# A graph layer and a routed feed-forward layer on one core: another order of the beginning, and the stores of the experts' outputs issued by SP

## The chip, the cores and the metric

The kernel runs on one core of a Trainium2 chip. The metric is the device time of one execution in microseconds (us). The core has a matrix engine (TensorE, PE in the profile), a vector engine (VectorE, DVE), an activation engine (ScalarE, ACT), a general engine (GpSimd, POOL) and SyncE (SP), which here does nothing but issue transfers. Each engine runs its own list of instructions in order; they wait for each other through semaphores.

## What is computed

The input `x` is 128 graphs of 64 nodes with 128 features, that is 8192 rows, and `adj` a 64x64 matrix for each graph. There are two layers, each behind a layer norm and a residual sum:

```python
def gnn(x, adj, ...):            # first layer
    h = layer_norm(x, ln_gamma, ln_beta)
    conv = (adj @ h) @ W_rel + b_rel + h @ W_root
    return x + relu(conv)
def ffn(x, ...):                 # second layer, 8 experts, the 2 best of each row
    scores = x @ Wg.T + bg
    combine = softmax over the two highest scores, 0 elsewhere
    for e in range(8):
        out += combine[e] * (relu(x @ W1[e].T + b1[e]) @ W2[e].T + b2[e])
x = x + gnn(_layernorm(x), adj, ...)
x = x + ffn(_layernorm(x), ...)
```

## The kernel before, in words

The 8192 rows are 64 tiles of 128 rows. Four tiles are a quad (16 quads, number n), and the quads fall into five groups (g) of 8, 16, 16, 16 and 8 tiles. Group 0 is quads 0 and 1, group 1 is quads 2 to 5.

A quad goes through the graph layer like this: `stats_in` and `scales_in` (DVE) make the scales of the layer norm; `norm_in` (DVE) or `h0_make` (ACT) normalizes into N; PE transposes (`h0_transpose`), ACT copies (`hT_copy`), PE multiplies (`relation`), ACT copies (`u_copy`), PE multiplies with the adjacency (`convolve`, semaphore conv_done). `plus_norm` (ACT) adds the normalized input into X, `residual` (DVE) adds the relu, `stats_out`, `scales_out_first` and `scales_out_last` make the next scales, `norm_out` normalizes, `split_high` (ACT) and `split_low` (DVE) make two half-precision parts XHL, `xn_transpose`, `xnT_copy` and `score` give the gate's scores, and `scores` (DVE, L466) copies them to LG.

For a group, DVE then picks the two best experts of each row (`route_first`, `route_second`), PE counts (`rank`), and DVE computes where each row goes (`route_slots`, `route_rows`, which ends with IDX, L543) and which expert each block has (`route_blocks`). POOL scatters the rows of the group, sorted by expert, to the DRAM tensor `rows` with two indirect DMAs for each tile (`scatter`, L317), and after the experts gathers their outputs from `yrows` in the same way (`gather`, L330). POOL's order is scatter 0, scatter 1, gather 0, scatter 2, scatter 3, gather 1, scatter 4, gathers 2, 3, 4. A scatter waits for zeros that SP wrote into `rows` (`zero_rows`).

The sorted rows are worked on in 84 blocks of 256 rows (number p; 12, 20, 20, 20 and 12 by group). For block p, PE computes `hidden(p)` (L990 to L992) as soon as SP has brought the rows in transposed (XT, `load_rows`, L244, four chunks of two blocks each), ACT and DVE make the two halves HH and HL (`high_half` L791, `low_half` L571), PE computes `output(p)` (L1006 to L1019) after `hidden(p+1)`, ACT copies it to YB (`y_copy`, L799), and once a chunk of two blocks is copied its 256 KB are stored to `yrows` (`store_y`). YB holds three chunks. The order of everything on each engine is written out by hand; the tables START, STATS, ROUTE and COMBINE say beside which block the later quads and groups get their steps.

Before the block loop comes the beginning. On PE it is: the graph layer of quads 0 to 3 up to `convolve`, the scores of quads 0 and 1, then the first experts' weights (`four_whole`, `four_rest`: 8 experts in two halves through the banks WB, each answered by `four_high` and `four_low` on ACT), then `first_half(4, 5)`, then the transposes and scores of quads 2 to 5. The second weights are split by `second_high` (ACT) and `second_low` (DVE, L580), one 512-column piece for each expert. `output(0)` waits for all eight of them (w2lo_made).

SP issues its transfers in one order too: `load_rows(ch)` of a chunk waits, for a group's first chunk, until the scatter of that group has landed, and from the fifth chunk on until the chunk that had the place has been read (hb_done).

Of the kernel before, what the change touches and what calls it, by code (L numbers as in the profile page):

```python
# [76 lines left out]
def build(nc, x, adj, wgn, w1, w2, b1, b2, kf, kh, out):  # L77
    ctx = ExitStack()
    with ctx:
# [71 lines left out]
        WB = 2 * [PA, PB, PH[0], PH[1]]  # L151
# [74 lines left out]
        def _(sp):  # L226
# [22 lines left out]

            def zero_rows(b):  # L250
                sp.wait_ge(zero_made, 1)
                sp.dma_start(rows[b].rearrange("(p n b) d -> p n (b d)", p=P, n=3),
                             ZERO.unsqueeze(1).to_broadcast([P, 3, ZW])).then_inc(zero_out[b], 16)
# [16 lines left out]
            zero_rows(0)  # L270
            for n in (4, 5):
                sp.wait_ge(conv_done, n - 3)
                load_adj(n)
            zero_rows(1)
# [9 lines left out]
            for ch in range(len(CH)):  # L284
# [5 lines left out]
                for n, at in COMBINE.items():  # L290
                    if ch == CB[at] + 6:
                        store_out(n)
            for n in range(NQ):
# [54 lines left out]
        def _(dve):  # L348
# [59 lines left out]
            def norm_in(n):  # L408
                g = group_of(n, Q0)
                if n >= 4:  # L410
                    dve.wait_ge(xnT_done, n - 3)
                    dve.wait_ge(xhi_made, n - 3)
                for k in range(GT):
# [211 lines left out]
            split_low(1)  # L625
            scores(0)
# [3 lines left out]
            norm_in(4)  # L630
            route_slots(0)
            route_rows(0)
            route_blocks(0)

            dve.wait_ge(b1hi_made, 1)
            nc.vector.scalar_tensor_tensor(B1L[:, :], B1F[:, :], W1S, B1H[:, :], ALU.mult, ALU.subtract).then_inc(b1lo_made, 1)
            dve.wait_ge(bt_made, 1)
            nc.vector.scalar_tensor_tensor(B2[32:33, :], B2F[32:33, :], YS / 64.0, BT[32:33, :],
                                           ALU.mult, ALU.subtract).then_inc(b2_made, 1)
            pair_of_quads(2)  # L640
            second_low(0, 1)
            split_low(2)
            split_low(3)
            second_low(1, 2)
            scores(2)
            second_low(2, 3)
            scores(3)
            pair_of_quads(4)
            second_low(3, 6)
            split_low(4)  # L650
            split_low(5)
            second_low(6, 7)
            scores(4)
            second_low(7, 8)
            scores(5)
            route_first(1)
            route_second(1)
# [47 lines left out]
        def _(act):  # L705
# [95 lines left out]
            def store_y(ch):  # L801
                g, r, w = chunk_rows(ch)
                act.wait_ge(y_made, CH[ch][1] + CH[ch][2])
                act.dma_start(yrows[g][r, :].rearrange("(k p) d -> p k d", p=P),
                              YB[:, ch % YR * CW:ch % YR * CW + w].rearrange("p (k d) -> p k d", d=P)).then_inc(y_out[ch % YR], 16)

# [22 lines left out]
            for n in (0, 1):  # L829
                xnT_copy(n)  # L830
            plus_norm(3)
            h0_make(5)
            four_high(0)
            exp_gap(0)
            four_low(0)
            four_high(4)
            four_low(4)
            act.wait_ge(b1_in, 16)
            nc.scalar.mul(B1H[:, :], B1F[:, :], W1S).then_inc(b1hi_made, 1)
            act.wait_ge(b2_in, 32)  # L840
            nc.scalar.activation(B2[0:1, :], B2F[0:1, :], ACT.Copy, scale=YS / 64.0).then_inc(b2_made, 1)
            nc.scalar.activation(BT[32:33, :], B2F[32:33, :], ACT.Copy, scale=YS / 64.0).then_inc(bt_made, 1)
# [4 lines left out]
            second_high(0, 4)  # L847
            norm_out(3)
            for n in (2, 3):
                split_high(n)  # L850
            for n in (2, 3):
                xnT_copy(n)
            for n in (4, 5):
                plus_norm(n)
            second_high(4, 8)
# [3 lines left out]
            for n in (4, 5):  # L859
                xnT_copy(n)  # L860
            act.wait_ge(b2_made, 2)

            for p in range(NP):
# [4 lines left out]
                for ch, (g, first, n) in enumerate(CH):  # L868
                    if p == first + n + 1:
                        store_y(ch)  # L870
# [23 lines left out]
            for ch, (g, first, n) in enumerate(CH):  # L894
                if first + n + 1 >= NP:
                    store_y(ch)
# [259 lines left out]
```

## Time and profile before

| what | value |
|---|---|
| median of 3 runs | 740.11 us (738.97 to 742.23) |
| the profiled execution | 739.89 us, its span 738.0 us |
| TensorE busy | 397.4 us, 54% of the span |
| VectorE, ScalarE, GpSimd busy | 310.2, 241.7 and 250.0 us |
| mean DMA rate | 81 GB/s |
| indirect DMAs of GpSimd | 256: 128 scatters, 128 gathers |

The page of the profile cuts the span into 40 equal slices and gives one digit for the busy share of each engine in each. The timeline lists instructions in order of time. A view by windows gives the busy time of each engine, with the number of its instructions, between two moments. "remote" or "another core or an unknown queue" stands where an engine waited and the profile names no engine that released it at that moment.

### The profile page before, as it was taken

Reading aid. Unit: us, or ns where it says so; the run is one execution under the profiler, and the core shown is the slowest. Engines: PE = TensorE matmul, PEld = TensorE weight load, DVE = VectorE, ACT = ScalarE, POOL = GpSimd, SP = SyncE. Lnnn points to the kernel's source line nnn. Section 1 sums busy time; section 2 is a strip of 40 time slices with the busy share of each in tenths; the row PEclk is TensorE's granted clock in tenths of the full one; section 3 lists DMA queues with packets and bytes.
Section 4 is the critical chain, followed back from the end, with each engine's and each line's share of the span. In section 5 each row is a group of like instructions: output and inputs, shape, how many; then the busy total and the mean of one; then the engine's idle time right before and its main releaser. Section 6 shows DMA issues by size and latency. Waiting matters only on the chain.

```text
span 738.0 us, 12242 instructions
## 1 busy us (share of the span) xinstructions
PE 397.4 (54%) x3927; PEld 332.7 (45%) x3927; DVE 310.2 (42%) x1113; ACT 241.7 (33%) x519; POOL 250.0 (34%) x263
## 2 busy tenths in 40 slices
PE   4873652199728505987211139964801999415910
PEld 4652540198618404875100039853701887314700
DVE  6773870067707403568400005761400753203651
ACT  3875310178425202852100027621300553102300
POOL 2043047400340672002777700044375000672053
PEclk9996585599868855999655559995955899756965
DMA  9934022132221211133111123232331442421231
GB/s 306 368 142 116 0 54 82 33 73 66 55 64 38 78 50 50 36 79 73 50 53 53 50 61 73 64 75 61 73 82 43 112 117 62 104 53 47 67 106 53
DMA packets 86540, 59.48 MB, mean 81 GB/s; under 512 B 57426, under 2 KB 78546, under 8 KB 85844
## 3 DMA queue, kind: packets, MB, share of 16 engines
q1 hardware_dynamic: 56756, 31.23, 14.7%
q0 software_dynamic: 8192, 16.79, 8.0%
q10 hardware_dynamic: 21536, 10.69, 6.1%
q8 instruction: 38, 0.62, 0.3%
q14 instruction: 18, 0.15, 0.1%
HBM read 19.61 MB, written 28.38 MB: 65 GB/s over the span
## 4 chain that ended last, share of the span: by engine, by line
PE 40%; another core or an unknown queue 23%; issue 19%; DVE 9%; ACT 5%; POOL 2%; DMA 1%; ACTq 0%; SPq 0%; DVEq 0%; POOLq 0%
PE PH L990 6%; PE PY L1014 5%; PE PY L1019 5%; PE PY L1015 5%; PE PH L992 5%; PE PH L991 4%; PE PY L1006 2%; POOL YG L330 2%; PE PB L911 1%; ACT N L734 1%; DVE STI L384 1%; PE PA L919 1%; DVE HL L571 1%; PE PA L920 1%
## 5 line engine op out<-in xcount | busy, mean ns | idle before, releaser
L571 DVE SCALAR_TENSOR_TENSOR HL<-PH,HH 128x512 f16<-128x512 f32 (+1 forms) x168 | 108.4, 674 | 293.0 <-ACT HH L791 244.5
L317 POOL DMA_INDIRECT rows<-XHL,IDX x128 | 123.9, 968 | 264.5 <-DVE IDX L543 227.0
L330 POOL DMA_INDIRECT YG<-yrows,IDX x128 | 121.8, 951 | 211.8 <-DMA yrows<-YB 173.9
L791 ACT ACTIVATE HH<-PH 128x512 f16<-128x512 f32 (+1 forms) x168 | 95.6, 582 | 145.3 <-remote 95.8
L1015 PE MATMUL PY<-W2H,HL 128*128 x652 | 122.6, 231 | 18.5 <-issue 18.4
L1014 PE MATMUL PY<-W2H,HH 128*128 x652 | 122.6, 231 | 10.9 <-issue 10.7
L990 PE MATMUL PH<-XT,W1H 128*128 128x256 f16 (+1 forms) x396 | 107.1, 273 | 26.6 <-issue 24.8
L799 ACT ACTIVATE YB<-PY 128x256 f32<-128x256 f32 x84 | 31.8, 378 | 272.7 <-remote 167.2
L992 PE MATMUL PH<-XT,W1L 128*128 128x256 f16 (+1 forms) x396 | 106.1, 271 | 20.5 <-issue 20.5
L1019 PE MATMUL PY<-W2L,HH 128*128 x652 | 106.6, 231 | 18.0 <-issue 18.0
L991 PE MATMUL PH<-XT,W1H 128*128 128x256 f16 (+1 forms) x396 | 106.3, 271 | 17.4 <-issue 17.4
L1006 PE MATMUL PY<-B,KH 128*128 x99 | 27.0, 272 | 110.5 <-issue 62.7
L1015 PEld LDWEIGHTS PY<-W2H,HL 128*128 128x128 f16 x652 | 67.8, 104 | 15.8 <-issue 15.0
L1014 PEld LDWEIGHTS PY<-W2H,HH 128*128 128x128 f16 x652 | 67.4, 103 | 15.7 <-issue 13.2
L1019 PEld LDWEIGHTS PY<-W2L,HH 128*128 128x128 f16 x652 | 57.1, 104 | 23.2 <-issue 22.7
L1006 PEld LDWEIGHTS PY<-B,KH 128*128 128x128 f16 x99 | 10.0, 101 | 120.3 <-issue 118.8
L990 PEld LDWEIGHTS PH<-XT,W1H 128*128 x396 | 41.2, 104 | 46.8 <-issue 37.4
L992 PEld LDWEIGHTS PH<-XT,W1L 128*128 x396 | 40.8, 103 | 25.3 <-issue 20.5
L991 PEld LDWEIGHTS PH<-XT,W1H 128*128 x396 | 40.9, 103 | 23.1 <-issue 19.2
L590 DVE SCALAR_TENSOR_TENSOR X<-YG,PR,X 128x128 f32<-128x128 f32 x128 | 36.2, 347 | 17.2 <-DMA YG<-yrows,IDX 16.6
L460 DVE SCALAR_TENSOR_TENSOR XHL<-N,XHL 128x512 f16<-128x512 f32 x16 | 10.8, 690 | 47.3 <-issue 30.7
L727 ACT ACTIVATE X<-X,SHI,SC 128x128 f32<-128x128 f32 x64 | 26.1, 483 | 0.0
(186 smaller groups left out, 517.8 us busy)
## 6 DMA issues: line engine op xcount, KB each, us to landing
yrows<-YB ACTq DMA_DIRECT2D x37, 256.0 KB, 2.7
rows<-XT SPq DMA_DIRECT2D x2, 2496.0 KB, 15.5
YG<-in_w SPq DMA_DIRECT2D x2, 2048.0 KB, 11.8
out<-X SPq DMA_DIRECT2D x16, 256.0 KB
X<-in_x SPq DMA_DIRECT2D x3, 1024.0 KB, 5.5
ADJ<-in_adj SPq DMA_DIRECT2D x32, 64.0 KB, 3.2
rows<-XHL,IDX POOLq DMA_INDIRECT x128
YG<-yrows,IDX POOLq DMA_INDIRECT x128
```

The costliest lines, as they stand in the source:

```text
L317: nc.gpsimd.indirect_dma_start(rows[g % 2], bass.IndirectOffsetOnAxis(ap=IDX[:, col:col + 1], axis=0), XHL[:, src:src + 2 * P].bitcast(F32 ...
L330: nc.gpsimd.indirect_dma_start(YG[g % 2][:, dst:dst + P], None, yrows[g], bass.IndirectOffsetOnAxis(ap=IDX[:, col:col + 1], axis=0)).then_ ...
L571: nc.vector.scalar_tensor_tensor(layer(HL[:, at:at + 2 * BW], p), layer(PH[p % 2 * 2 + h][:, :], p), 0.0, layer(HH[:, at:at + 2 * BW], p), ...
L590: ins = nc.vector.scalar_tensor_tensor(tile(X, t), y, PR[:, pr:pr + 1], tile(X, t), ALU.mult, ALU.add)
L791: nc.scalar.activation(layer(HH[:, at:at + 2 * BW], p), layer(PH[p % 2 * 2 + h][:, :], p), ACT.Relu).then_inc((hia_made, hib_made)[h], 1)
L990: nc.tensor.matmul(o, wh, hi, start=True, stop=False)
L991: nc.tensor.matmul(o, wh, lo, start=False, stop=False)
L992: last = nc.tensor.matmul(o, wl, hi, start=False, stop=True)
L1006: nc.tensor.matmul(PY[:, k * n * P:(k + 1) * n * P], KH[:, H_B2M:H_B2M + P], b2, start=True, stop=False, skip_group_check=True)
L1014: nc.tensor.matmul(o, HH[:, at:at + P], wh, start=False, stop=False, skip_group_check=True)
L1015: nc.tensor.matmul(o, HL[:, at:at + P], wh, start=False, stop=False, skip_group_check=True)
L1019: last = nc.tensor.matmul(o, HH[:, at:at + P], wl, start=False, stop=c == C - 1, skip_group_check=True)
```

## The change

The diff does five things:

1. `store_y` moves from ACT to SP. ACT issued the store of a chunk one block after its last copy, behind the two `high_half` of that block. SP issues it as soon as the copy is made; its loop over chunks (`next_chunk`) is cut into the first four chunks and then, block by block, the load of chunk ch+4 and the store of chunk ch.
2. On SP, `zero_rows(0)` stands after the adjacency loads of quads 4 and 5.
3. On PE, the graph layer of quads 4 and 5 up to `convolve` stands before the weights; the weights' banks (WB) and the waits that protect them are others.
4. On DVE, `norm_in(4)`, `residual`, `stats_out` and `scales_out` of quads 2 and 3 move around the routing of group 0; `residual` to `norm_out` of quads 4 and 5 stand before the scores of quads 2 and 3; six of the eight `second_low` and the low part of B2 stand after `route_second(1)`.
5. On ACT, the steps of quads 4 and 5 stand before `four_high(0)` or between the weights; the parts of B2 and six of the eight `second_high` come last.

```diff
 PH = [pb(f"PH{k}") for k in range(4)]
 PY = pb("PY")
 PA, PB, PC = pb("PA"), pb("PB"), pb("PC")
-WB = 2 * [PA, PB, PH[0], PH[1]]
+WB = [PB, PH[1], PH[3], PC, PB, PH[1], PY, PH[2]]
 
 def banks(n):
 
...
         sp.wait_ge(combined, n + 1)
         sp.dma_start(out[:, n * GW:(n + 1) * GW], X[:, n * GW:(n + 1) * GW]).then_inc(out_done, 16)
 
+    def store_y(ch):
+        g, r, w = chunk_rows(ch)
+        sp.wait_ge(y_made, CH[ch][1] + CH[ch][2])
+        sp.dma_start(yrows[g][r, :].rearrange("(k p) d -> p k d", p=P),
+                      YB[:, ch % YR * CW:ch % YR * CW + w].rearrange("p (k d) -> p k d", d=P)).then_inc(y_out[ch % YR], 16)
+
     def zero_rows(b):
         sp.wait_ge(zero_made, 1)
         sp.dma_start(rows[b].rearrange("(p n b) d -> p n (b d)", p=P, n=3),
...
     sp.dma_start(YG[1][:, :], w2[:, :]).then_inc(w2_in, 16)
     for r in (0, 32):
         sp.dma_start(B2F[r:r + 1, :], b2[:, :]).then_inc(b2_in, 16)
-    zero_rows(0)
     for n in (4, 5):
         sp.wait_ge(conv_done, n - 3)
         load_adj(n)
+    zero_rows(0)
     zero_rows(1)
 
     sp.wait_ge(b1hi_made, 1)
...
         load_x(g)
     for b in range(2):
         sp.wait_ge(zero_out[b], 16)
-    for ch in range(len(CH)):
+    def next_chunk(ch):
         load_rows(ch)
         for n, at in START.items():
             if ch == CB[at] + 2:
...
         for n, at in COMBINE.items():
             if ch == CB[at] + 6:
                 store_out(n)
+
+    for ch in range(XR):
+        next_chunk(ch)
+
+    for p in range(NP + 1):
+        for ch, (g, first, n) in enumerate(CH):
+            if p == first + n - 1 and ch + XR < len(CH):
+                next_chunk(ch + XR)
+            if p == first + n:
+                store_y(ch)
     for n in range(NQ):
         if n not in COMBINE or CB[COMBINE[n]] + 6 >= len(CH):
             store_out(n)
...
         if n >= 4:
             dve.wait_ge(xnT_done, n - 3)
             dve.wait_ge(xhi_made, n - 3)
+            dve.wait_ge(xlo_made, n - 3)
         for k in range(GT):
             t = n * GT + k
             at = 2 * T0[g] + GS[g] + t - T0[g]
...
     pair_of_quads(0)
     split_low(0)
     split_low(1)
+    norm_in(4)
     scores(0)
     scores(1)
     route_first(0)
     route_second(0)
-    norm_in(4)
+    residual(2)
+    stats_out(2, 0)
     route_slots(0)
     route_rows(0)
+    residual(3)
+    stats_out(3, 1)
+    scales_out_first(2, 2)
+    scales_out_last(2, 2)
+    norm_out(2)
     route_blocks(0)
 
     dve.wait_ge(b1hi_made, 1)
     nc.vector.scalar_tensor_tensor(B1L[:, :], B1F[:, :], W1S, B1H[:, :], ALU.mult, ALU.subtract).then_inc(b1lo_made, 1)
+    for i in range(2):
+        residual(4 + i)
+        stats_out(4 + i, i)
+    split_low(2)
+    split_low(3)
+    scales_out_first(4, 2)
+    scales_out_last(4, 2)
+    norm_out(4)
+    second_low(0, 2)
+    scores(2)
+    scores(3)
+    split_low(4)
+    split_low(5)
+    scores(4)
+    scores(5)
+    route_first(1)
+    route_second(1)
     dve.wait_ge(bt_made, 1)
     nc.vector.scalar_tensor_tensor(B2[32:33, :], B2F[32:33, :], YS / 64.0, BT[32:33, :],
                                    ALU.mult, ALU.subtract).then_inc(b2_made, 1)
-    pair_of_quads(2)
-    second_low(0, 1)
-    split_low(2)
-    split_low(3)
-    second_low(1, 2)
-    scores(2)
-    second_low(2, 3)
-    scores(3)
-    pair_of_quads(4)
-    second_low(3, 6)
-    split_low(4)
-    split_low(5)
-    second_low(6, 7)
-    scores(4)
-    second_low(7, 8)
-    scores(5)
-    route_first(1)
-    route_second(1)
+    second_low(2, 8)
 
     for p in range(NP):
         for n, at in START.items():
...
         at = ch % YR * CW + (p - CH[ch][1]) * BW
         nc.scalar.mul(YB[:, at:at + width(p)], PY[:, 0:width(p)], 1.0 / YS).then_inc(y_made, 1)
 
-    def store_y(ch):
-        g, r, w = chunk_rows(ch)
-        act.wait_ge(y_made, CH[ch][1] + CH[ch][2])
-        act.dma_start(yrows[g][r, :].rearrange("(k p) d -> p k d", p=P),
-                      YB[:, ch % YR * CW:ch % YR * CW + w].rearrange("p (k d) -> p k d", d=P)).then_inc(y_out[ch % YR], 16)
-
     act.wait_ge(b2_zero, 1)
 
     nc.scalar.activation(IDLE[:, :], B2[:, 0:1], ACT.Identity)
...
         split_high(n)
     for n in (0, 1):
         xnT_copy(n)
+    h0_make(5)
     plus_norm(3)
-    h0_make(5)
-    four_high(0)
-    exp_gap(0)
-    four_low(0)
-    four_high(4)
-    four_low(4)
-    act.wait_ge(b1_in, 16)
-    nc.scalar.mul(B1H[:, :], B1F[:, :], W1S).then_inc(b1hi_made, 1)
-    act.wait_ge(b2_in, 32)
-    nc.scalar.activation(B2[0:1, :], B2F[0:1, :], ACT.Copy, scale=YS / 64.0).then_inc(b2_made, 1)
-    nc.scalar.activation(BT[32:33, :], B2F[32:33, :], ACT.Copy, scale=YS / 64.0).then_inc(bt_made, 1)
     for n in (4, 5):
         hT_copy(n)
     for n in (4, 5):
         u_copy(n)
-    second_high(0, 4)
+    exp_gap(0)
+    plus_norm(4)
+    act.wait_ge(b1_in, 16)
+    nc.scalar.mul(B1H[:, :], B1F[:, :], W1S).then_inc(b1hi_made, 1)
+    four_high(0)
+    plus_norm(5)
+    four_low(0)
     norm_out(3)
     for n in (2, 3):
         split_high(n)
+    four_high(4)
+    four_low(4)
+    second_high(0, 2)
     for n in (2, 3):
         xnT_copy(n)
-    for n in (4, 5):
-        plus_norm(n)
-    second_high(4, 8)
     norm_out(5)
     for n in (4, 5):
         split_high(n)
     for n in (4, 5):
         xnT_copy(n)
+    act.wait_ge(b2_in, 32)
+    nc.scalar.activation(B2[0:1, :], B2F[0:1, :], ACT.Copy, scale=YS / 64.0).then_inc(b2_made, 1)
+    nc.scalar.activation(BT[32:33, :], B2F[32:33, :], ACT.Copy, scale=YS / 64.0).then_inc(bt_made, 1)
+    second_high(2, 8)
     act.wait_ge(b2_made, 2)
 
     for p in range(NP):
...
             exp_gap(1)
         high_half(p, 0)
         high_half(p, 1)
-        for ch, (g, first, n) in enumerate(CH):
-            if p == first + n + 1:
-                store_y(ch)
         for n, at in START.items():
             if p == at + 5:
                 xnT_copy(n)
...
             if p == at + 2:
                 exp_gap(g)
     y_copy(NP - 1)
-    for ch, (g, first, n) in enumerate(CH):
-        if first + n + 1 >= NP:
-            store_y(ch)
 
 @block.tensor
 def _(pe):
...
 
     def weight_whole(c):
 
-        if c >= 4:
+        if c == 3:
+            pe.wait_ge(rank_used, 1)
+        if c in (4, 5):
             pe.wait_ge(wlo_made, c - 3)
+        if c >= 6:
+            pe.wait_ge(conv_read, c - 3)
         nc.tensor.matmul(WB[c][0:P - 1, :], KF[:, K_M:K_M + P - 1], YG[0][:, c * HID:(c + 1) * HID],
                          start=True, stop=True).then_inc(w_done, 1)
 
...
         xn_transpose(n)
     for n in (0, 1):
         score(n)
+
+    pe.wait_ge(score_made, 2)
+    for n in (4, 5):
+        h0_transpose(n)
+    for n in (4, 5):
+        relation(n)
     pe.wait_ge(kh_in, 16)
+    rank(0)
+    for n in (4, 5):
+        convolve(n)
     pe.wait_ge(w1_in, 16)
-
-    pe.wait_ge(score_made, 2)
     four_whole(0)
-    rank(0)
     four_rest(0)
     four_whole(4)
     four_rest(4)
     pe.wait_ge(wlo_made, 8)
-    first_half(4, 5)
     for n in (2, 3):
-        if n == 3:
-            pe.wait_ge(rank_used, 1)
         xn_transpose(n)
     for n in (2, 3):
         score(n)
```

## Rows read from the trace of the kernel before

**Rows 1.** The page: slices of PE and POOL; the zeros' stores.
```profile
PE   4873652199728505987211139964801999415910
POOL 2043047400340672002777700044375000672053
...
rows<-XT SPq DMA_DIRECT2D x2, 2496.0 KB, 15.5
```
**Rows 2.** By windows: stretch; busy us and instructions of PE, PEld, DVE, ACT, POOL; clock; DMA; GB/s.
```profile
44.43:50.80 6.37, 3.24 (x24) 2.70 (x25) 4.33 (x15) 5.56 (x10) 4.99 (x5) 1.00 0.42 122
50.80:61.00 10.20, 5.04 (x40) 4.66 (x39) 6.97 (x32) 5.33 (x12) 7.69 (x8) 0.97 0.66 262
98.92:107.20 8.28, 6.60 (x58) 5.55 (x58) 7.09 (x33) 0.38 (x1) 6.45 (x7) 0.65 0.15 48
107.20:143.96 36.76, 4.91 (x16) 1.49 (x16) 1.38 (x2) 1.20 (x2) 24.28 (x26) 0.56 0.22 62
143.96:193.76 49.80, 44.73 (x518) 42.03 (x519) 35.89 (x149) 37.60 (x87) 0.00 (x1) 0.95 0.28 64
353.00:435.60 82.60, 9.52 (x41) 4.66 (x41) 6.98 (x22) 3.11 (x7) 55.56 (x59) 0.53 0.16 47
```
**Rows 3.** Timeline of POOL (start, duration): scatter 0's first and last, scatter 1's.
```profile
44.43 1.13 POOL L317 DMA_INDIRECT rows<-XHL,IDX  x1 [39.58 <-DVE IDX L543]
63.86 0.96 POOL L317 DMA_INDIRECT rows<-XHL,IDX  x1 [0.30 <-issue]
98.92 0.96 POOL L317 DMA_INDIRECT rows<-XHL,IDX  x1 [34.10 <-DVE IDX L543]
138.13 0.96 POOL L317 DMA_INDIRECT rows<-XHL,IDX  x1 [0.30 <-issue]
```
**Rows 4.** Timeline of PE and ACT in the two scatters.
```profile
64.34 0.37 PE L926 MATMUL PC<-KF,N 128*128 128x128 f32 x1 [0.96 <-issue]
67.45 0.59 ACT L758 COPY T<-PH 128x512 f32<-128x512 f32 x1 [6.19 <-remote]
110.02 0.27 PE L1019 MATMUL PY<-W2L,HH 128*128 x2 [1.18 <-issue]
143.96 0.38 ACT L799 ACTIVATE YB<-PY 128x256 f32<-128x256 f32 x1 [26.26 <-remote]
```
**Rows 5.** Timeline of DVE: group 0's IDX; a pair's residual, scales, norm_out; second_low.
```profile
43.96 0.17 DVE L543 CAST IDX<-SLF 128x16 int32<-128x16 f32 x1
71.81 0.68 DVE L424 SCALAR_TENSOR_TENSOR X<-PA,X 128x512 f32<-128x512 f32 x1
78.40 1.11 DVE L453 TENSOR_SCALAR N<-X,SCO,SHO 128x127 f32<-128x127 f32 x4
79.43 1.88 DVE L580 SCALAR_TENSOR_TENSOR W2L<-YG,W2H 128x512 f16<-128x512 f32 x3
48.40 1.27 DVE L638 SCALAR_TENSOR_TENSOR B<-HL,HH 1x1024 f16<-1x1024 f32 x1 [1.66 <-issue]
```
**Rows 6.** Timeline: the last scores before the loop on PE and DVE, group 1's IDX.
```profile
83.33 1.85 PE L935 MATMUL PH<-WF,T 128*128 128x8 f32 x8
85.22 0.19 DVE L466 COPY LG<-PH 128x32 f32<-128x32 f32 x1 [0.92 <-PE PH L935]
98.46 0.18 DVE L543 CAST IDX<-SLF 128x32 int32<-128x32 f32 x1
```
**Rows 7.** Timeline: a group's last copy and its store, twice; SP's second store of zeros.
```profile
187.32 0.28 ACT L799 ACTIVATE YB<-PY 128x128 f32<-128x128 f32 x1
190.54 0.37 ACTq L804 DMA_DIRECT2D yrows<-YB  x1
703.75 0.28 ACT L799 ACTIVATE YB<-PY 128x128 f32<-128x128 f32 x1 [1.42 <-PE PY L1019]
704.06 0.37 ACTq L804 DMA_DIRECT2D yrows<-YB  x1
...
22.55 3.95 SPq L252 DMA_DIRECT2D rows<-XT  x1
```

## The prediction

> **What bounds the kernel now.** I began with the slices of the page [rows 1]. PE is busy for about half of the span, yet not evenly: its digits are 9 in some stretches and 0 or 1 in others, and wherever POOL's digits stay at 6 or 7 for two slices and more, PE's fall to 0 to 2. So I cut the span at POOL's bursts of indirect DMAs. After scatter 1 begins at 98.92 us, PE does 58 matmuls in 8.28 us, and then 16 in 36.76 us; in the longest burst the rest is 41 in 82.60 us, against 518 in 49.80 us in a stretch without a burst [rows 2]. The timeline shows what the waiting is: PE's last matmul of block 2's output starts at 110.02, and ACT, which waits for nothing else, copies that output at 143.96, 5.8 us after the start of the burst's last DMA (138.13) [rows 3, 4]. So inside a burst signals from PE arrive later and later, and PE itself comes to a crawl after some 60 matmuls. That number recurs: 24 + 40 in scatter 0 up to 61.0 us, 58 in scatter 1 [rows 2]. What it is in the chip I can't read from these rows; that it happens is enough.
>
> The time is therefore the work between bursts, plus some 60 matmuls' worth in each, plus the rest of each burst. 256 indirect DMAs follow each other every 1.26 us or so (19.43 us for 15 steps, 39.21 for 31 [rows 3]), and the diff changes neither their number nor their grouping. What it can change is how early scatter 1 starts: from there on all instructions are the same but for the stores. The first question is thus when IDX of group 1 is made (98.46 to 98.64), which follows the scores of quad 5 at DVE (done 85.41) by 13.2 us of routing without a gap, the burst 0.28 us behind [rows 3, 6]. Call the end of those last scores S; before, S = 85.4.
>
> **Beginning, up to scatter 0.** PE takes the eight transposes, relations and convolutions of quads 4 and 5 before the weights; DVE trades `norm_in(4)` (behind group 0's routing) for `residual(2)` and its statistics. Group 0's slots wait on DVE's own chain and on `rank(0)`, which PE now does before the weights' first half rather than behind it. I count IDX of group 0 about 0.5 us earlier (43.5 instead of 44.1) and scatter 0's first DMA at 43.9 instead of 44.43 [rows 3, 5]. It could be 1 us later if ACT's copies hold `rank(0)`; both ends stay in the range. `zero_rows(0)` goes to about 22.5 us, where `zero_rows(1)` is issued now [rows 7], and has 21 us to land, where the zeros took 15.5 [rows 1]: at no cost. If that cover were gone, scatter 0 would start late by the lack.
>
> **Scatter 0 and what stands beside it.** The burst ends as before 19.4 us behind its start, and the engines it held were released at 67.45, 3.6 us behind its last DMA's start [rows 3, 4]; now that is 43.9 + 19.4 + 3.6 = 66.9. Before, the burst had beside it the convolutions of quads 4 and 5, and PE's allowance of some 60 matmuls was used up by them and the first transposes: at 64.34 it was still at quad 3's transposes. Behind the release came everything of a pair's chain: copies, scores 2 and 3, residual, scales, norm_out, scores 4 and 5: 18 us, from 67.45 to 85.41 [rows 4, 6].
>
> Now PE has beside the burst only some 18 matmuls of the weights, 8 transposes and 16 scores of quads 2 and 3, and 8 transposes of quads 4 and 5, 50 in all; 16 of quads 4 and 5's scores are left. DVE's chain needs nothing from PE after `convolve(5)`. From IDX at 43.5 it is residual and statistics of quad 3 (1.6), scales (3.5), norm_out (1.1), blocks of group 0 (2.7 with B1), residual and statistics of 4 and 5 (3.1), two split_low (1.3), scales (3.5), norm_out (1.1): 61.4 us. The parts come from the pair at 71.81 to 79.5, which is 6.6 us up to norm_out and 1.1 for it [rows 5]. So DVE is through about 5 us before the release. I expect quad 4 and 5's transposes issued but their signals held to 66.9. Then: ACT's copy 0.6, two scores of 1.9 at the half clock [rows 4, 6], DVE's copy 0.2 and hand-overs of 0.2: S = 71.4. That is 14.0 earlier. Bounds: if no signal is late, the chain itself ends at 66.8 (earliest S, 67); if ACT gets the scales of quads 4 and 5 only at the release, norm_out and split_high (2.8 us) come on top, S = 74.2. I take the middle case, since held signals are what the rows of scatter 0 show, and the half clock what PE has after idling.
>
> **What comes back.** The low part of B2 (1.27) and six `second_low` (1.88 for three, 3.8) now stand between `route_second(1)` and the first `low_half`, and so ahead of `route_slots(1)` on the same in-order engine [rows 5]: 5.1 us, of which nothing lies beside other work, because DVE has no gap from S to IDX. Behind it waits POOL, and `output(0)` on PE. ACT's six `second_high` lie beside DVE's routing and cost nothing. `hidden(0)` starts 4 us later relative to S, since it waits for B2, but PE idles there: `output(0)` waits for DVE in either case.
>
> Scatter 1 starts at 71.4 + 13.5 + 5.1 = 90.0 instead of 98.92: **8.9 us earlier**. At its start the loop stands where it stood (the same blocks done, since DVE's order from the first `low_half` on is the same), so all behind moves with it.
>
> **The stores by SP.** ACT loses 42 issues of 0.37 us [rows 7], which cost its activations nothing visible, as they were issued beside them; and ACT isn't the bound in the loop: 37.60 of 49.80 us, PE 44.73 [rows 2]. SP gets them in the order in which their causes occur: the load of chunk ch+4 needs `hidden` of a chunk's last block, the store its copy one block later, the next load the next `hidden`. At a group's end the store was 2.9 us behind the copy (190.54 against 187.60), and SP can issue it at once [rows 7], so gathers 0 to 3 start up to 3 us earlier. That gives nothing: a burst that begins earlier finds PE as much less far, and costs the same. At the very end the store already followed at once (704.06 against 704.03) [rows 7], and there alone it would count. I take 0, between -3 (if the earlier gathers shorten something that I don't see) and +3.
>
> Here the Trainium skill speaks against the change: DMA: Bandwidth & Descriptors, Queues, rings and completion order, says that SP and ACT own one ring each on every DMA engine, that a ring is worked through in order and that an engine takes turns between rings. A store on SP's ring would stand behind the transposing load and adjacency loads issued before it, where on ACT's it took its turn. No row here shows the two on one ring. By it the gathers come later than I say by some transfer, which changes the sum only at the end of the kernel, where SP has no loads left.
>
> **Sum.** Profiled execution 739.89 - 8.9 = 731.0; its own span would be 729.1. The median stands 0.2 above that execution, so 731.2.
>
> **Rivals.**
> A. *The beginning gains nothing and the routing is late* (slower). Place: DVE between S and IDX. If the weights' hand-overs between PE and ACT (`four_whole(4)`, `four_rest(4)`, all before quad 2's transposes now) get into the held signals of scatter 0, then transposes and scores 2 to 5 come behind the release, S stays near 85, and the 5.1 us are pure loss: 745. It decides at S = 80.3: above, the change is slower. For it: the hand-overs number 16, and the last come 10 us into the burst. Against: only 18 matmuls are in the queue by then, and after 24 in the first 6.4 us the engines still went at full speed [rows 2].
> B. *Half*: signals of DVE and ACT are held as well, S between 76 and 80: 736 to 740.
> C. *More*: nothing is held, S = 67, and something of the stores counts: 724 to 727.
> D. *SP blocks*: a store stands behind a group's first load, which waits for a scatter; YB's three chunks fill and ACT and PE stop. It needs the scatter to land more than three chunks after the load's turn. Scatter 1 was over before block 4's output, where that load's turn is block 5: it costs nothing. If it happened once for one chunk, two blocks of some 45 matmuls at 518 in 49.8 us [rows 2], 9 us, would come on top of the forecast: 740, and 749 at two of the four groups' ends.
>
> **How the numbers follow.** The forecast (S 68 to 76, 727 to 736) has 0.64, C 0.09, B 0.14, A 0.09, D 0.04. What a measurement can tell from no change is 0.5%, 3.7 us: faster below 736.4, slower above 743.8. Faster: 0.64 + 0.09 + a little of B = 0.75; within 0.5%: 0.13; slower, from A and D: 0.12. The range 725 to 740 leaves out the better part of C, and A and D. The likeliest case's own range is 727 to 736.
>
> **What would show it.** Right: scatter 0's first DMA near 44; LG of quad 5 (L466's sixth) near 71; scatter 1's first near 90, its 32 as long as before; ACT's first copy behind it near 135; gather 4's first near 698. The stores stand under SP's queue right behind their copy, with a landing near 2.7 us as now. Wrong: a sixth L466 past 76; IDX of group 1 more than 19 us behind it; scatter 1 at 90, but a later burst moved by less or more than 9 us, which would mean that the stores or the placing of a burst do count.

## Result: 1.26% faster, at the time that was forecast

In four executions each on one chip the changed kernel takes 731.28 us in the median (730.36 to 732.49) and the kernel before 740.67 us (738.97 to 742.23): a ratio of 0.9874, 95% interval 0.9851 to 0.9897. The profiled execution is 731.02 us with a span of 729.2 us. The forecast was 731.2 and 729.1. The agreement is in part luck: two terms of the working are wrong by about 3.5 us each, and they cancel. (The ratios here and below are those on record, each with its interval; they are not the plain quotients of the medians.)

**The page of the profile after.** First the slices of PE and POOL as in [rows 1], then two lines of its list of transfers: output and input, queue, operation, number, size, median us from issue to landing.

```profile
span 729.2 us, 12242 instructions
PE   4884541399477317885111159956613999306900
POOL 2044067200611770004777600062573000771052
...
yrows<-YB SPq DMA_DIRECT2D x37, 256.0 KB, 2.3
```

The picture is the one of before: wherever POOL stays at 6 or 7 for two slices and more, PE falls to 0 to 4. The stores stand on SP's queue and land after 2.3 us in the median (2.7 before, on ACT's), of those whose landing the profile has.

**The two scatters by windows** of the changed kernel, columns as in [rows 2]:

```profile
44.17:50.50 6.33, 4.71 (x13) 1.95 (x12) 5.61 (x29) 5.81 (x14) 4.99 (x5) 1.00 0.14 43
50.50:60.70 10.20, 6.08 (x24) 3.45 (x22) 6.83 (x28) 7.17 (x15) 7.69 (x8) 0.86 0.67 240
93.43:101.70 8.27, 6.31 (x57) 5.39 (x58) 7.12 (x33) 0.38 (x1) 6.44 (x7) 0.67 0.21 63
101.70:138.00 36.30, 5.22 (x17) 1.69 (x16) 1.38 (x2) 1.20 (x2) 24.33 (x26) 0.55 0.21 60
```

Scatter 1 has 57 matmuls in its first 8.27 us and 17 in the next 36.30; before it was 58 in 8.28 and 16 in 36.76 [rows 2]. The burst has moved and is otherwise the same.

**POOL's timeline after** (start, duration, line, what it does, idle time before and who ended it): scatter 0's first DMA, scatter 1's, gather 0's, gather 4's.

```profile
44.17 1.13 POOL L333 DMA_INDIRECT rows<-XHL,IDX  x1 [39.31 <-DVE IDX L560]
...
93.43 0.96 POOL L333 DMA_INDIRECT rows<-XHL,IDX  x1 [29.14 <-DVE IDX L560]
...
184.86 0.98 POOL L346 DMA_INDIRECT YG<-yrows,IDX  x1 [51.21 <-DMA yrows<-YB]
...
697.94 1.05 POOL L346 DMA_INDIRECT YG<-yrows,IDX  x1 [37.89 <-DMA yrows<-YB]
```

Scatter 1 is 5.5 us earlier than before (98.92 [rows 3]), not 8.9. Gather 0, which was at 193.76, is 8.9 us earlier, and gather 4, then at 706.93, is 9.0 us earlier. So the gain came in two places: 5.5 us in the beginning, and some 3.5 us more around gather 0. These are differences of one trace each, and such moments vary: over the twelve traces on record of kernels with the new beginning, scatter 0 starts between 43.6 and 45.8 us.

**DVE's timeline after**, inside scatter 0 and up to IDX of group 1: first and last steps of the scales of quads 4 and 5 with two of those between, LG of quad 5, IDX.

```profile
57.01 0.21 DVE L389 TENSOR_TENSOR MEANO<-STO 128x8 f32<-128x8 f32 x1
...
59.05 0.17 DVE L392 TENSOR_TENSOR MDIFO<-MDIFO 128x8 f32<-128x8 f32 x1 [1.68 <-remote]
...
61.14 0.17 DVE L453 TENSOR_SCALAR RAO<-VARO 128x8 f32<-128x8 f32 x1 [1.23 <-DVE VARO L393]
...
67.64 0.17 DVE L463 SCALAR_TENSOR_TENSOR SHO<-MEANO,SCO 128x8 f32<-128x8 f32 x1
...
74.67 0.19 DVE L483 COPY LG<-PH 128x32 f32<-128x32 f32 x1 [1.51 <-PE PH L947]
...
92.97 0.18 DVE L560 CAST IDX<-SLF 128x32 int32<-128x32 f32 x1
```

From the fourth step of the scales on each needs the result of the one ahead of it on DVE, and many start late by up to 1.68 us for a step of 0.17 us (the profile names DVE's own step as what ended the wait in seven cases, of 0.33 to 1.23 us; for the longest it names none). The scales take 10.8 us (57.01 to 67.81) where 3.5 were counted. The last scores are done at 74.86, and IDX follows 18.3 us later.

**ACT's and SP's timeline after**: ACT's `norm_out` of quad 5, its first copy behind scatter 1, then a group's last copy and its store, the next block's copy, and the last group's pair.

```profile
67.85 1.65 ACT L758 ACTIVATE N<-X,SHO,SCO 128x127 f32<-128x127 f32 x4 [6.11 <-DVE SHO L463]
...
138.53 0.38 ACT L823 ACTIVATE YB<-PY 128x256 f32<-128x256 f32 x1 [26.25 <-remote]
...
181.69 0.28 ACT L823 ACTIVATE YB<-PY 128x128 f32<-128x128 f32 x1
181.99 0.38 SPq L253 DMA_DIRECT2D yrows<-YB  x1
...
199.03 0.38 ACT L823 ACTIVATE YB<-PY 128x256 f32<-128x256 f32 x1 [11.26 <-remote]
...
694.75 0.28 ACT L823 ACTIVATE YB<-PY 128x128 f32<-128x128 f32 x1 [1.46 <-PE PY L1035]
695.05 0.36 SPq L253 DMA_DIRECT2D yrows<-YB  x1
```

Block 11, the last of group 0, is copied 5.6 us earlier than before (187.32 [rows 7]). Its store is issued 0.02 us behind the copy's end instead of 2.94. Numbering the copies by block, the changed kernel leads the one before by 5.5 us at block 0, 5.6 at block 11, 7.9 at 13 (12 itself, held inside gather 0's burst, is 4.3 us later), 9.5 at 14, about 9.9 at 19 to 31, about 11.1 at 35 to 52 (behind the burst with gather 1), 9.4 at 58 and 9.0 from 67 to the end, but for single blocks that a burst holds. So the second half of the gain appears in blocks 12 to 14, under gather 0.

### The profile page after: what moved, and what is told of

It is laid out like the page before. It is cut to its first block, busy times and chain, and to the rows that moved or that the text cites. A ratio compares the mean times of both kernels' runs of the same rounds, so it can differ in the third digit from the quotient of the medians.

```text
span 729.2 us, 12242 instructions
## 1 busy us (share of the span) xinstructions
PE 396.6 (54%) x3927; PEld 333.3 (46%) x3927; DVE 310.9 (43%) x1113; ACT 241.1 (33%) x519; POOL 249.4 (34%) x263
## 4 chain that ended last, share of the span: by engine, by line
PE 35%; another core or an unknown queue 26%; issue 17%; DVE 13%; ACT 5%; POOL 2%; DMA 1%; SPq 0%; DVEq 0%; ACTq 0%; POOLq 0%
PE PH L1006 5%; PE PY L1030 5%; PE PY L1035 5%; PE PY L1031 5%; PE PH L1008 4%; PE PH L1007 4%; POOL YG L346 2%; PE PY L1022 2%; PE PB L923 2%; DVE HL L588 1%; ACT N L758 1%; ACT N L740 1%; DVE STO L447 1%; DVE STI L400 1%
## 5 line engine op out<-in xcount | busy, mean ns | idle before, releaser
L1030 PEld LDWEIGHTS PY<-W2H,HH 128*128 128x128 f16 x652 | 67.8, 104 | 21.1 <-issue 18.5
L607 DVE SCALAR_TENSOR_TENSOR X<-YG,PR,X 128x128 f32<-128x128 f32 x128 | 36.2, 347 | 18.5 <-DMA YG<-yrows,IDX 16.8
L477 DVE SCALAR_TENSOR_TENSOR XHL<-N,XHL 128x512 f16<-128x512 f32 x16 | 10.8, 688 | 38.4 <-issue 24.7
```

The costliest lines, as they stand in the source:

```text
L607: ins = nc.vector.scalar_tensor_tensor(tile(X, t), y, PR[:, pr:pr + 1], tile(X, t), ALU.mult, ALU.add)
L1030: nc.tensor.matmul(o, HH[:, at:at + P], wh, start=False, stop=False, skip_group_check=True)
```

## The experiments

Twelve runs were made on four chips, on each together with the kernel before, and the chips differ: on two the kernel before takes 739.8 and 746.1 us, on two others 480.0 and 480.5. On the latter PE keeps its pace beside the indirect DMAs. So a gain in us is compared only on one chip. Experiments 1 to 6 ran on the kind without the crawl, and what they say holds for that kind.

**1. The beginning alone** (new beginning, `store_y` on ACT as before).

```diff
-            if p == first + n:
-                store_y(ch)          # SP, and its loop by blocks
+    for ch in range(len(CH)):
+        next_chunk(ch)               # SP as before
...
+        for ch, (g, first, n) in enumerate(CH):
+            if p == first + n + 1:
+                store_y(ch)          # ACT as before
```

> The changed kernel with the stores of the experts' outputs back on ACT, one block later, as before; the new beginning alone. Theory 1 (the beginning gave the 5.5 us by which scatter 1 starts earlier, and the stores the rest): 5.5 us faster than before, 735; gather 0 again 6 us behind the group's last copy, copies 14 and later 5 to 7 us ahead of before. Theory 2 (the stores give nothing and the beginning gives all, as the prediction had it): 731, copies from number 14 on 9 to 10 us ahead.

475.17 us against 480.0: ratio 0.9876 (0.9850 to 0.9901).

**2. The stores alone** (beginning as before; SP's `store_y` and its loop as in the change).

> The kernel before with the stores moved to SP, its own beginning kept; the stores alone. Theory 1: gather 0 starts some 3.3 us earlier than before, copies 0 to 11 unmoved, copies 14 and later 3 to 4 us ahead, time 737. Theory 2: 740, no copy moved by more than 1 us.

477.95 us: 0.9946 (0.9915 to 0.9978). On this chip both parts gain alone.

**3. The stores at once, but by ACT.**

```diff
+                    if p == first + n:
+                        store_y(ch)  # ACT, right behind y_copy(p - 1)
```

> The changed kernel, but ACT issues each store, right behind the copy that completes the chunk and not one block later. Tells the earlier moment of the store from the engine that issues it. If the moment counts (a gather starts earlier): within 1 us of the changed kernel, 731. If the other queue or ACT's relief counts: near the kernel with the stores back on ACT, 734 to 735.

478.41 us: 0.9970 (0.9938 to 1.0002), 3.2 us slower than experiment 1, with earlier stores. So ACT cannot take the earlier issue for nothing. The traces don't show where the 3.2 us are: the profiled execution of experiment 3 is its fastest (476.46 us), that of experiment 1 its slowest (477.31). (In 200 to 250 us PE starts 493 matmuls in the one and 521 in the other, but over the whole span the one with fewer is ahead.) ACT waits for its own copy before it issues, ahead of its next `high_half`; that this is the reason was only argued.

**4. A pause before gather 1**, meant to cut the burst of 64 DMAs there in two.

```diff
     scatter(3)
+    pool.wait_ge(y_made, 38)
     gather(1)
```

> The changed kernel, with POOL waiting for the copy of block 37 between scatter 3 and gather 1, so that the burst of 64 indirect DMAs becomes two of 32. If each burst leaves PE some 60 matmuls before it crawls (an allowance that a pause renews), PE gains about 5 us: 726. If what a burst costs is simply its length, no change: 731. If gather 1 then meets what needs it, slower.

475.01 us: 0.9872 (0.9846 to 0.9899). Nothing crawls on this chip, so it couldn't test the allowance of 60 matmuls. Nor did POOL pause: block 37 is copied at 282.6 us, while scatter 3 is still being issued, and the 112 DMAs from 253.98 to 394.01 us run on without a gap. So this is in effect one more measure of the changed kernel.

**5 and 6. The changed kernel again, with experiment 1 beside it**, on another chip, which proved to be of the same kind.

> The changed kernel once more, beside a run of the kernel before on the same chip. The four kernels run last took 475 to 478 us where before took 480, without the crawl of PE beside the indirect DMAs; so it is to be seen what the change is worth where there is no crawl. If the crawl is there (before near 740): 731, as measured. If it is not (before near 480): the beginning brings scatter 0's end and S forward and costs 5 us of second weights; by the kernel with the new beginning alone 475, and if the stores by SP add what they alone gave (2 us), 473.

> The new beginning with the stores left on ACT, in one call with the changed kernel. Theory 1 (stores count through the earlier gather 0): with the crawl 735 against 731 of the changed kernel, gather 0 some 3 us later relative to the copies; without the crawl 475 against 473. Theory 2 (the stores give nothing): the two agree within 1 us in either case.

474.70 us, 0.9890 (0.9860 to 0.9920), and 476.24 us, 0.9917 (0.9887 to 0.9947), against 480.53: the stores' part is 1.5 us here, within the intervals. The use of the run is its trace. First the windows of scatter 1, then DVE's first and last step of the scales of quads 4 and 5, of the changed kernel on this chip:

```profile
87.80:96.00 8.20, 7.12 (x70) 6.54 (x71) 7.65 (x34) 2.22 (x5) 6.37 (x7) 0.67 0.34 95
96.00:132.00 36.00, 26.02 (x321) 24.17 (x319) 21.96 (x81) 25.01 (x58) 24.56 (x26) 0.89 0.24 69
```
```profile
58.44 0.20 DVE L389 TENSOR_TENSOR MEANO<-STO 128x8 f32<-128x8 f32 x1
61.72 0.17 DVE L463 SCALAR_TENSOR_TENSOR SHO<-MEANO,SCO 128x8 f32<-128x8 f32 x1
```

It is the same program with the same 26 DMAs in 36 us, and 321 matmuls beside them instead of 17. The scales take 3.45 us instead of 10.8. The last scores are done at 69.22 and IDX of group 1 at 87.49, so the way from scores to IDX is again 18.3 us. The steps of the chain were counted rightly; what was left out is how far the crawl reaches. The beginning isn't worth more here for all that, as the old one isn't held either: scatter 1 starts at 90.58 in experiment 2 and at 87.71 in experiment 1, on one chip.

The next six ran on chips with the crawl.

**7. Six `second_low` behind IDX** (the 5.1 us that come back: are they on the path by themselves?).

```diff
-    second_low(2, 8)
...
     route_rows(1)
+    second_low(2, 8)
```

> The changed kernel with its last six second_low behind the routing of group 1 (IDX) and not ahead of it. If the second weights' 3.7 us stood on the path to scatter 1, scatter 1 starts 3.7 us earlier. Theory 1 (POOL's start is what counts): 3 to 4 us faster where PE crawls beside the bursts, and without the crawl 0 to 1 us faster, since there the end hangs on PE and on POOL from scatter 3 on. Theory 2 (the blocks count, not POOL): output(0) now waits for these six, so 1 to 2 us slower.

733.65 us: 0.9914 (0.9888 to 0.9941). Scores to IDX stays at 18.2 us. DVE's timeline has the reason, its first `low_half`:

```profile
83.07 0.69 DVE L588 SCALAR_TENSOR_TENSOR HL<-PH,HH 128x512 f16<-128x512 f32 x1 [2.94 <-ACT HH L815]
```

DVE now idles 2.94 us, and 0.53 us more before the next `low_half`: ACT's HH needs `hidden(0)`, and that needs the low part of B2, which DVE makes only behind `route_second(1)`. The cover of the one is the other.

**8. Late, only the last store of groups 0 to 3**, and **9. late, all the others.**

```diff
+    def late(ch):
+        return ch < len(CH) - 1 and (ch + 1 in C0)      # 9: "not in"
...
-    sp.wait_ge(y_made, CH[ch][1] + CH[ch][2])
+    sp.wait_ge(y_made, CH[ch][1] + CH[ch][2] + late(ch))
...
-            if p == first + n:
+            if p == first + n + late(ch):
```

> The changed kernel with the stores of the last chunks of groups 0 to 3 alone issued one block later (SP still issues them); all other stores as in the changed kernel. Theory 1 (the stores count only through the start of the gather behind them): as slow as the kernel with the stores on ACT, that is 476 to 477 without the crawl, 734 to 735 with it. Theory 2 (the stores count by another queue, or ACT's relief): as the changed kernel, 474.7 or 731.

> The reverse: the stores of all chunks but each group's last issued one block later by SP, the last ones at once. Theory 1: as the changed kernel, 474.7 without the crawl, 731 with it. Theory 2: as slow as the kernel with the stores on ACT, 476 or 735.

736.67 us, 0.9959 (0.9930 to 0.9988), and 731.48 us, 0.9878 (0.9851 to 0.9906). With the four stores at the groups' ends late the kernel is 5.2 us slower than with the other 38 late. Timelines of ACT, SP and POOL: the last copy of group 0, its store, gather 0, the copy of block 15; first of 8, then of 9.

```profile
182.95 0.28 ACT L826 ACTIVATE YB<-PY 128x128 f32<-128x128 f32 x1
191.05 0.38 SPq L256 DMA_DIRECT2D yrows<-YB  x1
194.20 0.97 POOL L349 DMA_INDIRECT YG<-yrows,IDX  x1 [59.35 <-DMA yrows<-YB]
225.90 0.39 ACT L826 ACTIVATE YB<-PY 128x256 f32<-128x256 f32 x1 [0.85 <-PE PY L1038]
```
```profile
182.93 0.28 ACT L826 ACTIVATE YB<-PY 128x128 f32<-128x128 f32 x1
183.23 0.38 SPq L256 DMA_DIRECT2D yrows<-YB  x1
186.09 0.97 POOL L349 DMA_INDIRECT YG<-yrows,IDX  x1 [52.02 <-DMA yrows<-YB]
221.84 0.38 ACT L826 ACTIVATE YB<-PY 128x256 f32<-128x256 f32 x1 [0.85 <-PE PY L1038]
```

Both stand at the same place at block 11. Gather 0 is 8.1 us earlier in 9, and four blocks later 9 is 4.1 us ahead. The 38 late stores cost nothing that can be seen (0.9878 here, 0.9874 for the change on another chip), so as far as these runs tell the stores act through the start of a gather. The 5.2 us aren't what the change gained by them, though: gather 0 begins 11.3 us behind the start of the last copy in 8, against 6.4 in the kernel before.

**10 and 11. B2 made early, without and with experiment 7's move.**

```diff
+    # DVE: B2's low part before scores(4); ACT: its two parts before norm_out(5)
+    nc.vector.scalar_tensor_tensor(B2[32:33, :], B2F[32:33, :], ...)
     scores(4)
...
     route_second(1)
-    nc.vector.scalar_tensor_tensor(B2[32:33, :], B2F[32:33, :], ...)
-    second_low(2, 8)                 # 11 only: to behind route_rows(1)
```

> B2's parts early alone, second_low where the change has it. Theory 1: the second weights are then the bound on DVE, S to IDX 17.0 us (18.3 less the 1.2 of B2's low part), scatter 1 1.2 us earlier, 730. If B2 alone was the hold: as good as with both moved.

> The changed kernel with both things that stand between S and scatter 1 taken away: B2's parts early (ACT while it waits for the scales of quads 4 and 5, DVE ahead of scores(4)), and the six second_low behind IDX. Theory 1 (two covers: the second weights on DVE, and the first hidden that waits for B2; each hides the other, as the kernel with second_low alone moved showed 18.2 us from S to IDX in both): S to IDX falls to 13.3 us, scatter 1 4.9 us earlier, with the crawl 726 to 727; without it 473 to 475, as there the end hangs on later work of POOL. Theory 2 (something else holds the routing): S to IDX stays at 17 us and more, 731.

Number 10 takes 734.49 us, 0.9849 (0.9819 to 0.9878); number 11 takes 736.52 us, 0.9864 (0.9836 to 0.9892). Scores to IDX is 16.8 us in 10 and 13.2 in 11: all 5.1 us are gone in 11, where scatter 1 starts at 90.70 against 93.66 in 10. Yet 11 isn't faster than 10. Windows of scatter 1 with ACT's copy of block 3 behind it, first of 10, then of 11:

```profile
93.70:102.00 8.30, 6.62 (x59) 5.48 (x59) 7.07 (x33) 0.38 (x1) 6.47 (x7) 0.67 0.27 79
102.00:139.00 37.00, 4.88 (x15) 1.52 (x15) 1.38 (x2) 1.19 (x2) 24.17 (x26) 0.55 0.19 55
...
142.73 0.38 ACT L823 ACTIVATE YB<-PY 128x256 f32<-128x256 f32 x1 [0.74 <-PE PY L1035]
```
```profile
90.70:99.00 8.30, 4.45 (x37) 3.96 (x37) 6.19 (x16) 0.00 (x0) 6.47 (x7) 0.59 0.16 49
99.00:136.00 37.00, 7.67 (x37) 3.94 (x37) 4.87 (x23) 1.68 (x4) 24.44 (x26) 0.53 0.15 46
...
143.60 0.38 ACT L823 ACTIVATE YB<-PY 128x256 f32<-128x256 f32 x1 [0.85 <-PE PY L1035]
```

Both do 74 matmuls in the burst. But when it begins 302 have been started in 11 and 339 in 10, since in 11 `output(0)`, which needs all `second_low`, comes only then. The burst begins 3.0 us earlier with 37 matmuls fewer behind it, and block 3's copy is 0.9 us later.

**12. The beginning alone**, as experiment 1, on the chip of 10 and 11.

> The new beginning alone, stores on ACT and one block later as before. The kernel with only the groups' last stores late lost 5 us to the changed one where PE crawls (736.7 against 731.5 in one call). With the stores as in the kernel before, gather 0 begins 6.4 us behind the last copy and not 11.3: with the crawl 734 to 735; without it 476.

739.73 us against 746.06: 0.9906 (0.9874 to 0.9937), that is -6.3 us. Its last copy of group 0 and gather 0:

```profile
185.50 0.28 ACT L810 ACTIVATE YB<-PY 128x128 f32<-128x128 f32 x1
...
191.85 0.97 POOL L333 DMA_INDIRECT YG<-yrows,IDX  x1 [55.46 <-DMA yrows<-YB]
```

Gather 0 begins 6.4 us behind the start of that copy, as before (6.4 [rows 7] and 193.76), against 3.2 in the changed kernel. This trace is of the slowest of the six executions (742.32 us), and scatter 1 starts at 96.29 in it, not at 93.4: on this chip the scales of quads 4 and 5 take 12.1 us, and S, the end of the last scores, is 77.7.

## Why the prediction came out, step by step

**What bounds the kernel: right in the main.** The slices were read too simply: beside POOL's stretches of 6 and 7 PE's digits in the kernel before are 0 to 5, not 0 to 2, the high ones in the first slice of a stretch.

**Beginning, up to scatter 0: right.** 43.9 was forecast and 44.17 measured, 0.26 us earlier than before, which is less than this moment varies between traces (43.6 to 45.8). The zeros cost nothing.

**The end of the last scores, S: mis-sized.** The step said that DVE's chain inside the burst runs as fast as outside it, "DVE is through about 5 us before the release", so that S = 71.4 (its terms add up to 71.7). The scales ended at 67.8, with the release, because DVE's waits for its own steps are held too: 10.8 us for the scales on this chip, 12.1 to 12.3 on that of experiments 10 to 12, 3.45 where nothing crawls. S is 74.9. The bound in the text, "if ACT gets the scales of quads 4 and 5 only at the release ... S = 74.2", is what happened (ACT's `norm_out` at 67.85), with 0.7 us on top. I had read the crawl as one of signals from PE, and took the middle case instead of the bound. Price: 3.5 us. The trace of before could mislead here. Its scatter 0 has the same chain, for quads 2 and 3, and it isn't held:

```profile
52.83 0.17 DVE L373 TENSOR_TENSOR MEANO<-STO 128x8 f32<-128x8 f32 x1
...
56.31 0.17 DVE L446 SCALAR_TENSOR_TENSOR SHO<-MEANO,SCO 128x8 f32<-128x8 f32 x1
```

That is 3.65 us, from 8.4 to 12.1 us behind the burst's start. In the changed kernel the first held step (59.05, due at 57.4) comes 13.2 us behind it. The chain of quads 4 and 5 was placed just where the holding begins.

Of DVE's steps the Trainium skill (VectorE: DVE Perf Modes, The DRAIN you can't avoid) reports that in a chain of copies a semaphore after each cost nothing extra. No run here leaves the semaphores out, so none tests that. What the traces show is the chain with them: starts 0.2 us apart where nothing is held, and up to 1.8 us apart in scatter 0.

**What comes back: the size right, the reason half.** 5.1 us were forecast between S and IDX beside the 13.2; 18.3 came. I put them all on DVE's own instructions. Experiment 7 shows that behind the six `second_low` stands a second cause of almost the same length, `hidden(0)` waiting for B2. I had written that its late start costs nothing since `output(0)` waits anyway; but DVE's routing stands behind a `low_half` that needs it. With the `second_low` moved alone 0.1 us goes, with B2 early alone 1.5 us (experiment 10), with both all 5.1 (experiment 11).

**Scatter 1 at 90.0: wrong, 93.43.** By the same working with S = 74.9 it is 93.5. Its 32 DMAs take as long as before, and ACT's first copy behind it, at 138.53, is 5.4 us earlier than before [rows 4]; 135 was forecast.

**The stores at 0: wrong, about -3.5 in these two traces.** The step that failed is "a burst that begins earlier finds PE as much less far, and costs the same". It takes for granted that a burst which begins 3 us earlier leaves 3 us of the work undone at its end. At a group's end it doesn't. The windows between the last copy of group 0 and gather 0, of the burst's first 8.2 us, and of the 17 us behind it: first before, then after.

```profile
187.60:193.80 6.20, 2.65 (x33) 2.31 (x31) 5.63 (x27) 3.08 (x7) 0.04 (x1) 0.98 0.42 95
193.80:202.00 8.20, 8.09 (x61) 7.08 (x60) 5.41 (x19) 3.63 (x8) 6.37 (x7) 0.60 0.17 45
...
213.00:230.00 17.00, 11.45 (x102) 11.17 (x103) 5.85 (x15) 8.28 (x19) 0.75 (x1) 0.67 0.16 40
```
```profile
182.00:184.90 2.90, 0.96 (x9) 0.61 (x7) 2.49 (x16) 0.21 (x1) 0.04 (x1) 1.00 0.42 109
184.90:193.10 8.20, 6.62 (x48) 5.95 (x49) 5.40 (x20) 2.87 (x7) 6.37 (x7) 0.66 0.34 84
...
204.00:221.00 17.00, 14.10 (x136) 12.69 (x136) 9.01 (x27) 10.21 (x23) 0.61 (x1) 0.78 0.17 40
```

Before, 6.2 us passed ahead of the burst with PE at 33 matmuls; DVE was busy for 5.63 us with scales of later quads, a `residual`, a `low_half` and statistics. After, the gap is 2.9 us, and the rest of that DVE work falls into the burst's first 8.2 us, in which it isn't held. DVE's timeline has the same steps, from this `residual` to the scales after it, first before (the burst starts at 193.76), then after (184.86); both take 4.6 to 4.8 us:

```profile
190.24 0.69 DVE L424 SCALAR_TENSOR_TENSOR X<-PA,X 128x512 f32<-128x512 f32 x1
...
194.82 0.16 DVE L369 SCALAR_TENSOR_TENSOR SCO<-RTO,SCO 128x4 f32<-128x4 f32 x1
```
```profile
184.57 0.69 DVE L441 SCALAR_TENSOR_TENSOR X<-PA,X 128x512 f32<-128x512 f32 x1
...
189.19 0.16 DVE L385 SCALAR_TENSOR_TENSOR SCO<-RTO,SCO 128x4 f32<-128x4 f32 x1
```

PE pays for the shorter gap first: from the last copy to 8.2 us into the burst it starts 57 matmuls instead of 94. It makes that up later, with 17 against 9 in the rest of the burst and 136 against 102 in the 17 us behind it: 210 in 39.0 us after, 205 in 42.4 us before. That DVE's slow stretch beside the start of the burst is the reason is read from these rows, and no run took it alone.

From the copy of block 11 to that of block 15 it takes 42.5 us before, 41.3 in experiment 12 and 43.0 in 8, the kernels with a late last store; it takes 38.4 after and 38.6 to 39.2 in experiments 7, 9, 10 and 11, with a prompt one. That is the gain around gather 0, and the start of the gather switches it. Its size over the whole kernel is less sure: the beginning alone has a ratio of 0.9906 and the change 0.9874 (on two chips, the intervals overlap), and the difference of 0.3% is 2.4 us. Experiments 8 and 9 show on one chip that late group ends cost time (5.2 us), but with more delay than the kernel before had. The text had named -3 as the lower end, "if the earlier gathers shorten something that I don't see", and "scatter 1 at 90, but a later burst moved by less or more than 9 us" as a sign that the stores count; they do, though scatter 1 wasn't at 90.

That gather 1 adds 1.3 us and the stretch of gather 2 takes 1.8 back isn't explained.

**An allowance of some 60 matmuls per burst: right for scatter 1, not shown to be a count.** Scatter 1 has 57 in its first 8.3 us, and 59 in experiment 10. Experiment 11 has 37 in the same time, because `output(0)` wasn't ready, and so got nothing for its earlier start. But in gather 0 of the changed kernel the crawl follows on 48, and in scatter 0 the first step is held when PE has started 26, 13.2 us into the burst; before, ACT was first held 13.7 us into it, with 56. The moment recurs better than the number, and what PE gets done until then is what lies ready.

**ACT's freed issues at nothing: open in part.** Experiment 3 shows that prompt stores on ACT cost about 3 us where nothing crawls; late ones, as the kernel before had them, measured 1.5 us slower than SP's there, inside the intervals (experiments 5 and 6).

**Stores on SP's queue behind its loads: no wait seen.** Landing on SP's queue takes 2.0 to 3.5 us, 2.3 in the median, against 2.3 to 4.0 and 2.7 on ACT's.
By the Trainium skill (DMA: Bandwidth & Descriptors, Queues, rings and completion order) SP and ACT each have a ring of their own on every DMA engine, worked through in ring order; from this it would follow that a store on SP's ring stands behind the loads issued there before it. No wait of that kind shows in these landings.

**Rivals.** A decided at S = 80.3 and S was 74.9. B was right in its cause, "signals of DVE and ACT are held as well", with S short of its 76 to 80 here; on the chip of experiments 10 to 12 S is 76.6 to 77.7, inside them. But what it priced at 736 to 740 didn't come: experiment 12, with S = 77.7 and nothing from the stores, has a ratio of 0.9906, which is 734 us beside 740.67. C needed S = 67, which only the chips without the crawl have (67.1 to 69.2). D didn't occur: all 42 stores are issued 0.02 to 0.03 us behind their copy, so SP was never blocked.

**A better version.** Experiment 10, the change with B2 made early, has the best ratio, 0.9849; the change has 0.9874, on another chip, and the intervals overlap, so whether it is faster than the change stays open.

**What stays open.** What holds the engines in a burst, and why on some chips only, can't be read from these traces. The stores alone (experiment 2) weren't tried where the crawl is, and a pause before gather 1 that POOL really waits for wasn't tried at all. With one trace of each kernel, how much of the 5.5 us at scatter 1 is variation stays open too; counted from the start of scatter 0 they are 5.2 us, and 4.0 on the chip of experiment 12 against the same trace of before.

## What to carry to other kernels

Where a burst of one engine slows all the others, ask what each engine has ready in its first microseconds and which slow stretch it can cover, not only how early it is; here a gather that began as soon as its inputs were ready gained time at a group's end. Before counting a step free because it waits for something else anyway, look for a second wait of the same length, since an edit that takes away one alone can give next to nothing. Look where in a burst a chain will fall, and not only whether such a chain was slow there before. And when a total agrees with the forecast, compare it at every stage: here 3.5 us too few and 3.5 too many made one right number.

## What the runs showed of the hardware

- One program takes 480 us on two chips and 740 to 746 us on others. In the 36 us behind the first 8 of scatter 1, with 26 indirect DMAs in each, PE starts 321 matmuls on a chip of the first kind and 17 on one of the second.
- In a burst on the second kind an engine's wait for its own preceding instruction is held too: up to 1.2 us (1.7 where the profile names no cause) for DVE's steps of 0.17 us, which start 0.2 us apart otherwise.
- The first 8 us of scatter 1 are not slowed in this way: DVE is busy for 7.12 us of 8.27, PE starts 57 matmuls. In scatter 0 the holding begins 13 to 14 us behind the burst's start, whether PE has started 26 matmuls (the changed kernel) or 56 (the one before).
